# Projections and causal convolution of the next tile moved into the level steps of a gated delta layer

## The chip, the cores and the metric

The kernel runs on one core of one Trainium2 chip. The metric is the device time of one launch in microseconds. The unchanged kernel takes 6232.35 us, the median of 3 runs (6223.12 to 6238.5).

## The reference

Two residual blocks work on x of shape (4, 1024, 128) in fp32. The first is a gated delta attention with 6 heads, keys and queries of 128, values of 32. The second is a stack of 6 layers of local attention and a feed-forward part, which the change doesn't touch. The part that the change touches computes, for the normalised x:

```python
q = _causal_conv_silu(x @ Wq, conv_q)   # depthwise, 4 taps over time, then silu
k = _causal_conv_silu(x @ Wk, conv_k)
v = _causal_conv_silu(x @ Wv, conv_v)
beta = sigmoid(x @ Wb); g = -exp(A_log) * softplus(x @ Wa + dt_bias)
q = _l2norm(q) * DK ** (-0.5); k = _l2norm(k)
def step(S, inp):                        # over the 1024 positions
    q_t, k_t, v_t, g_t, b_t = inp
    S = S * exp(g_t)
    u = (v_t - einsum('bhk,bhkv->bhv', k_t, S)) * b_t
    S = S + k_t * u
    return S, einsum('bhk,bhkv->bhv', q_t, S)
o = o * rsqrt(mean(o * o) + EPS) * norm_w * silu(x @ Wg)
x = x + o @ Wo
```

The projections have 768 + 768 + 192 columns, which are 14 chunks of up to 128 channels.

## The kernel before, in words

`delta_layer` handles the 1024 positions in 8 tiles of 128 positions by 4 batches, so that most operands are 128 partitions by 512 columns. A loop over t from -1 to 8 builds one block of instructions for each engine, and a barrier of all engines (line 899) ends each block. The block t = -1 only normalises tile 0. The block t = 8 only finishes tile 7. The eight blocks between do one tile each. `behind` (t >= 1) means that the output of the tile before is still to be projected and added; `ahead` (t < 7) means that the next tile's x is to be loaded, turned and normalised.

The order within a block is written out by hand, and each engine works through its own list in order. Semaphores tie the lists together. In this account "head of a tile" is everything up to the first level step:

- PE projects the 14 chunks of the convolution (line 316) into four banks in turn. ACT copies each chunk into `pre` behind three columns kept from the tile before (line 523), and writes the last tap to `cv` (line 531). DVE adds the other three taps (line 735), two chunks interleaved. ACT applies silu (line 536). POOL's `tensor_copy` puts the kept columns in front of a chunk (line 639) and keeps the new ones (line 642). In between, the old tile's output is scaled (`squares_o`, `gated_o`, lines 686 to 695), turned and projected (`turn_o`, `output`), added (`residual`, line 699) and normalised (`mean_1`, `variance(LAST_LN)`).
- PE computes the gates (line 322), ACT applies silu to them (line 552) and changes its table to Ln and Exp (line 555). DVE then works off a chain of small dependent operations for the decay and beta (lines 750 to 776, called the gate chain here; line 761 is the first that needs ACT's exponentials, L561). Behind it stand the masked decays (line 781) and the 12 scalings of q and k (line 791).
- POOL squares q and k (line 649), PE sums them (line 342).

Then follow three pairs of heads. For a pair, the inverse of a 128 by 128 triangular matrix is built in six levels i = 1 to 6. At each level and for each of the two heads (x = 0, 1), PE forms one product (line 412, four matrices, each an fp32 product of two instructions), ACT copies it (`p1`, line 614), PE forms two further products (lines 433 and 436), and DVE subtracts them from `tr` and `tt` (lines 854 and 856). POOL prepares the masked blocks `ao` (line 660), up to two levels early. It waits for `at_ready` at level 1 of a pair and for an earlier product of line 412 at the others. In pairs 0 and 1, levels 1 and 3 also hold the decay products of the next heads (lines 352, 353), levels 2 and 4 their key products (lines 362, 363), and DVE `weigh`s them after levels 2 and 4 (lines 802 to 810). DVE's `first_t` (lines 817, 822) comes before level 6. In pair 2 the same slots hold `turn_x`, `mean_x` and `variance(NEXT_LN)`.

Between two pairs lies a passage: PE reads the states (lines 443, 445), turns A of the next heads (`turn_a`, line 370, taken to `at` by ACT, line 573), and waits for DVE's `r_ready` (lines 873 to 877) before the product of line 455. Then come the outputs and state updates (lines 463, 465), `turn_k` (line 376), and the next pair's first product of line 412.

## Time and profile before

The profiled execution took 6223.25 us, its span 6221.4 us. The delta layer occupies the span up to about 2280 us.

| what | value |
|---|---|
| PE busy | 5319.4 us, 86% of the span |
| DVE busy | 4155.1 us, 67% |
| ACT busy | 2763.5 us, 44% |
| POOL busy | 2394.6 us, 38% |
| mean granted TensorE clock | 0.924 of full speed |
| delta layer, tiles start (t = 0 to 8) | 27.9, 296.4, 578.6, 859.5, 1141.8, 1422.7, 1705.0, 1985.9, 2267.0 us |

Busy times are sums over the engine's instructions. The tile starts are the first table loads of line 501 after each barrier. The span in slices shows PE at five to eight tenths in the delta layer and at nine tenths behind it, with a granted clock of seven to nine tenths in the first part. PEclk is given in tenths or as a share; 1.00 is 2.4 GHz and 0.50 is 1.2 GHz.

### The profile page before, as it was taken

The page shows a single profiled execution, that of the slowest core. Times are in us where ns is not written, and L with a number is a line of the kernel's source. Part 1 is how long each engine was busy: PE and PEld are TensorE (multiplying, and loading weights), DVE is VectorE, ACT ScalarE, POOL GpSimd, SP SyncE. Part 2 cuts the span into 40 slices and gives each one's busy share as a digit, 9 for nine tenths or more (in the row PEclk, how much of TensorE's full clock was granted, in tenths as well). Part 3 has the DMA queues.
Part 4 walks back from the last instruction along what each step waited for, and adds up shares of the span by engine and source line. Part 5 has one row for each costly group of instructions (what it writes and reads, how often), then busy time and mean ns, then how long its engine had stood idle before and what let it go on. Part 6 is the DMA issues. An engine that isn't in the chain of part 4 may idle for free. (4 is left out here: it accounts for less than half of the span.)

```text
span 6221.4 us, 170219 instructions
## 1 busy us (share of the span) xinstructions
PE 5319.4 (86%) x71376; PEld 3399.9 (55%) x71376; DVE 4155.1 (67%) x6338; ACT 2763.5 (44%) x5037; POOL 2394.6 (38%) x2148
## 2 busy tenths in 40 slices
PE   5878778686968768999999999999999999999994
PEld 4856657584857654444444555545444445445552
DVE  6565665556565657777777777777777777777772
ACT  4232231413132315555555555555555555555552
POOL 2232222222222215444444444444444444444440
PEclk8888888797878879999999999999999999999997
DMA  0000000000000002222222222222222222222221
GB/s 20 3 2 4 1 4 1 4 1 4 3 2 3 1 32 67 60 60 68 63 60 60 70 68 60 60 70 67 58 53 70 64 56 60 65 72 58 58 58 34
DMA packets 255841, 252.14 MB, mean 41 GB/s; under 512 B 29680, under 2 KB 248688, under 8 KB 254704
## 3 DMA queue, kind: packets, MB, share of 16 engines
q1 hardware_dynamic: 255088, 241.29, 15.4%
q8 instruction: 571, 9.36, 0.6%
q14 instruction: 182, 1.49, 0.1%
HBM read 29.90 MB, written 4.19 MB: 5 GB/s over the span
## 5 line engine op out<-in xcount | busy, mean ns | idle before, releaser
L1360 POOL TENSOR_TENSOR turn<-prod 128x512 f32<-128x512 f32 x768 | 983.0, 1280 | 1944.4 <-DVE prod L1400 1002.2
L1103 PE MATMUL banks<-w2s,xs 128*128 128x512 f32 x2304 | 1242.0, 622 | 97.2 <-DVE xs L1432 89.7
L1400 DVE TENSOR_TENSOR prod<-banks,tabs 128x1024 f32<-128x1024 f32 x768 | 935.6, 1218 | 114.1 <-ACT sq L1247 113.9
L1247 ACT ACTIVATE sq<-banks 128x512 f32<-128x512 f32 x768 | 458.6, 597 | 963.0 <-PE banks L1103 959.2
L1369 POOL TENSOR_TENSOR turn<-turn,rs 128x512 f32<-128x512 f32 x768 | 832.7, 1105 | 88.2 <-ACT rs L1264 84.2
L660 POOL TENSOR_TENSOR ao<-at,msk 128x512 f32<-128x512 f32 x288 | 388.0, 1358 | 1045.7 <-PE banks L412 564.2
L1133 PEld LDWEIGHTS banks<-msk,turn 128*128 128x128 f32 x3072 | 324.3, 140 | 572.4 <-issue 566.2
L1436 DVE TENSOR_REDUCE mx<-banks 128x8 f32<-128x512 f32 x384 | 265.5, 691 | 385.5 <-PE banks L1119 383.0
L1411 DVE TENSOR_REDUCE ss<-sq 128x8 f32<-128x512 f32 x768 | 518.8, 676 | 1.5
L854 DVE TENSOR_TENSOR tr<-tr,banks 128x512 f32<-128x512 f32 x240 | 165.1, 688 | 510.4 <-PE banks L436 509.1
L614 ACT ACTIVATE p<-banks 128x512 f32<-128x512 f32 x288 | 172.0, 597 | 722.4 <-PE banks L412 722.4
L1133 PE MATMUL banks<-msk,turn 128*128 128x128 f32 x3072 | 482.6, 280 | 3.4 <-ACT ot L1292 1.6
L1103 PEld LDWEIGHTS banks<-w2s,xs 128*128 128x128 f32 x2304 | 352.7, 193 | 149.8 <-DVE xs L1432 98.5
L1119 PE MATMUL banks<-kx,qt 64*32 64x64 f32 x24576 | 352.3, 224 | 89.1 <-issue 88.9
L412 PE MATMUL banks<-tr,ao 128*128 128x128 f32 x2304 | 345.9, 299 | 93.0 <-DVE tt L856 58.1
L1181 PE MATMUL banks<-ot,w2s 128*128 128x512 f32 x768 | 394.3, 595 | 3.8 <-ACT ot L1292 3.8
L1119 PEld LDWEIGHTS banks<-kx,qt 64*32 64x32 f32 x24576 | 274.2, 105 | 183.7 <-issue 183.4
L412 PEld LDWEIGHTS banks<-tr,ao 128*128 128x128 f32 x2304 | 308.2, 209 | 120.9 <-DVE tt L856 80.9
L1208 PE MATMUL banks<-xf,w2s 128*128 128x512 f32 (+1 forms) x576 | 296.9, 626 | 89.6 <-ACT msk L1321 59.7
L1286 ACT ACTIVATE pt<-banks 128x512 f32<-128x512 f32 x384 | 229.2, 597 | 311.6 <-PE banks L1140 311.6
L1158 PE MATMUL banks<-v,pt 64*32 64x66 f32 x24576 | 332.9, 225 | 2.7 <-ACT pt L1286 2.7
L1446 DVE RECIPROCAL rc<-banks 128x8 f32<-128x8 f32 x384 | 78.4, 204 | 382.5 <-PE banks L1158 382.4
(202 smaller groups left out, 9828.7 us busy)
## 6 DMA issues: line engine op xcount, KB each, us to landing
v<-v_tok SPq DMA_DIRECT2D x1152, 132.0 KB
v<-v_tok SPq DMA_DIRECT2D x384, 66.0 KB
v<-v SPq DMA_DIRECT2D x188, 132.0 KB, 2.5
w2s<-in_weights SPq DMA_DIRECT2D x10, 768.0 KB, 4.7
tabs<-in_rot SPq DMA_DIRECT2D x40, 128.0 KB, 2.7
w2s<-in_weights SPq DMA_DIRECT2D x1, 2713.5 KB, 11.0
w2s<-in_weights SPq DMA_DIRECT2D x10, 256.0 KB, 3.0
xin<-in_x SPq DMA_DIRECT2D x8, 256.0 KB, 2.9
```

Of the source, the lines that this page charges most:

```text
L412: last = pe.matmul(p[3 * x][:, b * P:(b + 1) * P], ao[:, 2 * x + i % 2, b, :], tr[:, x, b, :], start=True, stop=True)
L660: g.tensor_tensor(ao[:, 2 * x + i % 2, :, :], at[:, x, :, :], over_batches(msk[:, M_OFF + LEVELS + i, :]), ALU.mult)\
L1103: pe.matmul(a_bank(use), xs[:, t % 2, b * P:(b + 1) * P], w[:, at:at + 512], start=True, stop=True).then_inc(a_done, 1)
L1119: last = pe.matmul(sc[n * WIN:(n + 1) * WIN, h, b * 2 * WIN:(b + 1) * 2 * WIN], qt[r, j, b * P + n * WIN:b * P + (n + 1) * WIN], kx[r, j, ...
L1133: last = pe.transpose(turn_bank[:, i * P:(i + 1) * P], src[:, i * P:(i + 1) * P], ident)
L1158: last = pe.matmul(pv[n * WIN:(n + 1) * WIN, h, b, :], pt[r, g % 2, b * P + n * WIN:b * P + (n + 1) * WIN], v2[r, h2, b, n, i * DV1:(i + 1 ...
L1181: pe.matmul(out_bank, w[:, W_O + j * P:W_O + (j + 1) * P], ot[:, g % 3, :], start=(j == 0), stop=(j == NP2 - 1)).then_inc(o_done, 1)
L1247: a.activation(sq[:, r % 2, :], a_bank(use), ACT.Square).then_inc(sq_done, 1)
L1360: gp.tensor_tensor(turn[:, r % ROTS, :, :].rearrange(halves, s=2), prod[:, r % 2, 0, :, :].rearrange(halves, s=2), prod[:, r % 2, 1, :, :] ...
L1369: gp.tensor_tensor(turn[:, r % ROTS, :, :], turn[:, r % ROTS, :, :], along(rs[:, q % 2, b, :], DH), ALU.mult).then_inc(rot_done, 1)
L1400: v.tensor_tensor(prod[:, r % 2, :, :, :], a_bank(use).rearrange("p (h d) -> p h d", h=HU).unsqueeze(1) .to_broadcast([P, 2, HU, DH]), tab ...
L1411: v.tensor_reduce(ss[:, q % 2, b, :], sq[:, r % 2, :].rearrange("p (h d) -> p h d", h=HU), AX.X, ALU.add).then_inc(red_done, 1)
```

## The change

The 14 chunks of tile t + 1 are projected, taken, convolved and their last columns kept inside the level steps of tile t: chunk number `pair * 6 + i - 1`, so one chunk at each level until 14 are done (pair 2 has chunks 12 and 13). POOL handles chunk `pair * 6 + i - 2`, after its `ao` products of level i. The unactivated results stay in a second half of `acts`, and ACT applies silu to all 14 at the head of the next tile. The x of the next tile is turned and normalised in the head rather than in pair 2, and the old tile's output is scaled in the head (`squares_o`) and pair 1 (`gated_o`) and projected, added and normalised in pair 2. The chunks' banks are p[1] and p[4], so the product of line 433 goes to p[0] and p[3]. `pre` has two buffers for four. Tile 0's chunks are done in the block t = -1. The memset of `acts` is twice as wide, and that of `cv` goes. Several scratch tiles become views of others.

The diff, cut to what matters for the order and the waits:

```diff
-PRE = 4
+PRE = 2
...
         state = sb("state", [P, H1, NB, DV])
         xin = sb("xin", [P, NB, P])
...
-                v.memset(cv[:], 0.0)
+                v.memset(acts[:], 0.0)
                 v.memset(state[:], 0.0).then_inc(init_done, 1)
...
             attend, behind, ahead = 0 <= t < NT, t >= 1, t + 1 < NT
-            LAST_LN, NEXT_LN = 1, 1 + behind
+            NEXT_LN, LAST_LN = 1, 1 + ahead
+            act_qkv, conv = acts[:, t % 2, :, :], acts[:, (t + 1) % 2, :, :]
+            o, o_old = os[:, t % 2, :, :], os[:, (t - 1) % 2, :, :]
...
+                    def project(n):
+                        m = P if n < NCH - 1 else VD - P
+                        if n == 0:
+                            pe.wait_ge(xn_ready, 1)
+                        if n >= 2:
+                            pe.wait_ge(tap_ready, n - 1)
+                        pe.matmul(p[CONV_BANKS[n % 2]][0:m, :], w[:, n * P:n * P + m], xn[:], start=True, stop=True)\
+                            .then_inc(proj_ready, 1)
 
...
+                            for n in range(NCH):
+                                project(n)
...
-                    for n in range(NCH):
-                        m = P if n < NCH - 1 else VD - P
-                        if behind and n == 4:
-                            turn_o()
-                        if behind and n == 6:
-                            output()
-                        if behind and n == 8:
-                            mean_1()
-                        if n >= 4:
-                            pe.wait_ge(tap_ready, n - 3)
-                        pe.matmul(p[n % 4][0:m, :], w[:, n * P:n * P + m], xn[:], start=True, stop=True)\
-                            .then_inc(proj_ready, 1)
...
+                    if ahead:
+                        turn_x()
+                        mean_x()
+                        variance(NEXT_LN, p[2])
 
                     pe.wait_ge(silu_ready, NCH)
-                    if behind:
-                        pe.wait_ge(rstd_ready, LAST_LN)
                     for b in range(NB):
...
+                    if ahead:
+                        pe.wait_ge(xn_ready, 1)
+                    pe.wait_ge(ln_done, NQK)
...
-                            elif ahead and pair + 1 == H1 // 2:
+                            chunk = pair * (LEVELS - 1) + i - 1
+                            if ahead and chunk < NCH:
+                                if i <= 2 and pair:
+                                    pe.wait_ge(u_taken, 2 * pair)
+                                project(chunk)
+                            if behind and pair + 1 == H1 // 2:
                                 if i == 1:
-                                    turn_x()
+                                    turn_o()
                                 elif i == 2:
-                                    mean_x()
-                                elif i == 4:
-                                    variance(NEXT_LN, p[6])
+                                    output()
+                                elif i == 3:
+                                    mean_1()
+                                elif i == 5:
+                                    variance(LAST_LN, p[7])
                             for x in range(2):
...
-                                        pe.matmul(p[3 * x + 1][:, b * P:(b + 1) * P], tt[:, x, b, :],
+                                        pe.matmul(p[3 * x][:, b * P:(b + 1) * P], tt[:, x, b, :],
...
+                            if ahead:
+                                pe.wait_ge(tap_ready, min(NCH, (pair + 1) * (LEVELS - 1)))
...
-                    for n in range(NCH + PRE):
-                        if behind and n == 4:
-                            take_o()
-                        if behind and n == 10:
-                            square(LAST_LN)
-                        if n < NCH:
-                            take(n)
-                        if n >= PRE:
-                            silu(n - PRE)
-                        if n < NCH:
-                            last_tap(n)
+
...
                     a.wait_ge(gates_ready, 1)
                     for i in range(2):
                         src = p[4 + i][:, 0:2 * GW].rearrange("p (b n) -> p b n", b=2)
                         a.activation(sg[:, t % 2, 2 * i:2 * i + 2, :], src[:, :, 0:VD], ACT.Silu)\
                             .then_inc(gates_taken, 1)
-                    a.wait_ge(silu_ready, NCH)
+                    for n in range(NCH):
+                        a.activation(act_qkv[:, n, :], act_qkv[:, n, :], ACT.Silu).then_inc(silu_ready, 1)
+                        if ahead and n == 3:
+                            take_x()
+                        if ahead and n == 9:
+                            square(NEXT_LN)
                     a.preload_act_table_set(LN_EXP)
-                    if behind:
-                        rstd(LAST_LN, p[7])
+                    if ahead:
+                        rstd(NEXT_LN, p[2])
 
...
+                    if ahead:
+                        a.wait_ge(xn_ready, 1)
...
-                            if ahead and not more:
+                            chunk = pair * (LEVELS - 1) + i - 1
+                            if ahead and chunk < NCH:
+                                take(chunk)
+                                last_tap(chunk)
+                            if behind and pair == 1 and i == 1:
+                                inverse_o()
+                            if behind and not more:
                                 if i == 1:
-                                    take_x()
-                                elif i == 3:
-                                    square(NEXT_LN)
-                                elif i == 5:
-                                    rstd(NEXT_LN, p[6])
+                                    take_o()
+                                elif i == 4:
+                                    square(LAST_LN)
+                                elif i == 6:
+                                    rstd(LAST_LN, p[7])
...
+                    if not attend:
+                        if ahead:
+                            for n in range(NCH):
+                                keep_tail(n)
+                        return
...
+                            chunk = pair * (LEVELS - 1) + i - 2
+                            if ahead and 0 <= chunk < NCH:
+                                keep_tail(chunk)
...
+                    def convolve(n):
+                        m = P if n < NCH - 1 else VD - P
+                        v.wait_ge(pre_ready, n + 1)
+                        v.wait_ge(front_ready, n + 1)
+                        v.wait_ge(tap_ready, n + 1)
+                        dst = blocks(conv[0:m, n, :])
+                        for tap in range(KS - 1):
+                            if tap:
+                                v.wait_ge(conv_step, n * (KS - 2) + tap)
+                            v.scalar_tensor_tensor(dst, pre[0:m, n % PRE, :, tap:tap + P], cw[0:m, n, tap:tap + 1],
+                                                   dst, ALU.mult, ALU.add)\
+                                .then_inc(conv_step if tap < KS - 2 else conv_ready, 1)
...
+                            for n in range(NCH):
+                                convolve(n)
+                            v.wait_ge(conv_ready, NCH)
...
-                    for pair in range(0, NCH, 2):
-                        v.wait_ge(pre_ready, pair + 2)
-                        v.wait_ge(front_ready, pair + 2)
-                        v.wait_ge(tap_ready, pair + 2)
-                        for tap in range(KS - 1):
-                            for n in (pair, pair + 1):
-                                m = P if n < NCH - 1 else VD - P
-                                if tap:
-                                    v.wait_ge(conv_step, tap_count(n, tap - 1))
-                                dst = blocks(cv[0:m, n % PRE, :])
-                                ins = v.scalar_tensor_tensor(dst, pre[0:m, n % PRE, :, tap:tap + P],
-                                                             cw[0:m, n, tap:tap + 1], dst, ALU.mult, ALU.add)
-                                ins.then_inc(conv_step if tap < KS - 2 else conv_ready, 1)
-                        if behind and pair == 0:
-                            gated_o()
-                        if behind and pair == 4:
-                            residual()
-                        if behind and pair == 6:
-                            centre(LAST_LN, x1[:])
-                    v.wait_ge(conv_ready, NCH)
...
+                    if ahead:
+                        v.wait_ge(xt_ready, 1)
+                        centre(NEXT_LN, xt_new, p[3])
+                        normed(NEXT_LN, blocks(xn[:]))
+                    if behind:
+                        squares_o()
...
-                    if behind:
-                        normed(LAST_LN, last_block())
...
-                                    v.tensor_tensor(tr[:, x, :, :], tr[:, x, :, :], blocks(p[3 * x + 1]),
+                                    v.tensor_tensor(tr[:, x, :, :], tr[:, x, :, :], blocks(p[3 * x]),
...
+                            chunk = pair * (LEVELS - 1) + i - 1
+                            if ahead and chunk < NCH:
+                                convolve(chunk)
+                            if behind and pair == 1 and i == 4:
+                                gated_o()
+                            if behind and not more:
                                 if i == 2:
-                                    v.wait_ge(xt_ready, 1)
-                                    centre(NEXT_LN, xt[:, (t + 1) % 2, :])
-                                elif i == LEVELS - 1:
-                                    normed(NEXT_LN, blocks(xn[:]))
+                                    residual()
+                                elif i == 3:
+                                    centre(LAST_LN, x1, p[7])
+                                elif i == 6:
+                                    normed(LAST_LN, last_block())
```

## Rows read from the trace of the kernel before

**Rows 1.** The table by stretches, tile 4; columns: stretch, length, busy times, PEclk.
```profile
1141.84:1191.80 49.96, 25.35 (x52) 11.27 (x53) 37.18 (x58) 32.41 (x57) 14.81 (x30) 0.70 0.04 11
1191.80:1243.74 51.94, 34.22 (x118) 20.85 (x118) 34.96 (x69) 20.99 (x37) 16.44 (x14) 0.73 0.00 0
1243.74:1306.08 62.34, 55.76 (x432) 54.32 (x433) 38.55 (x66) 11.02 (x19) 17.18 (x13) 0.88 0.00 1
```

**Rows 2.** Timeline, end of tile 4's head; columns: start, length, engine, line, operation.
```profile
1189.02 1.28 ACT L555 ACT_TABLE_LOAD   x1
...
1191.81 0.45 PE L332 MATMUL banks<-msk,act_qkv 128*128 128x128 f32 x1 [14.37 <-ACT lrs L483]
...
1192.11 0.18 DVE L761 TENSOR_SCALAR t<-t 128x24 f32<-128x24 f32 x1 [1.07 <-ACT t L561]
```

**Rows 3.** Timeline, start of the kernel, first block and first tile.
```profile
2.66 6.03 DVE L227 MEMSET act_qkv<- 128x7168 f32 x1 [1.44 <-issue]
...
18.75 2.08 PE L271 MATMUL banks<-xt,msk 128*128 128x512 f32 x2 [0.69 <-ACT xt L489]
...
24.45 0.69 ACT L482 ACTIVATE llg<-banks,cst 128x512 f32<-128x512 f32 x1 [2.17 <-PE banks L275]
...
67.21 0.18 DVE L761 TENSOR_SCALAR t<-t 128x24 f32<-128x24 f32 x1 [0.59 <-ACT t L561]
```

**Rows 4.** Groups by line in the delta layer; columns: shapes, count, busy, mean ns.
```profile
L536 ACT ACTIVATE act_qkv<-cv 128x512 f32<-128x512 f32 x112 | 70.3, 628 | 36.0 <-DVE cv L735 34.6
...
L322 PE MATMUL banks<-w1s,xn 128*128 128x204 f32 x64 | 12.5, 338 | 0.0
...
L688 DVE TENSOR_TENSOR sg<-sg,rows 128x768 f32<-128x768 f32 x8 | 7.6, 948 | 0.0
```

**Rows 5.** Line 735's instructions: duration in ns, minimum, median, maximum.
```profile
L735 DVE SCALAR_TENSOR_TENSOR cv<-pre,cw,cv x336: 733/745/1531, 33.0 to 2030.4; 128x512 f32<-128x512 f32 x168
```

**Rows 6.** Timeline of PE, a level without extras, then a 512-column product.
```profile
1283.79 1.06 PE L412 MATMUL banks<-tr,ao 128*128 128x128 f32 x8
1285.33 1.16 PE L412 MATMUL banks<-tr,ao 128*128 128x128 f32 x8 [0.48 <-DVE tt L856]
...
1289.90 1.06 PE L412 MATMUL banks<-tr,ao 128*128 128x128 f32 x8
...
1378.21 1.02 PE L271 MATMUL banks<-xt,msk 128*128 128x512 f32 x2
1379.07 1.05 PE L433 MATMUL banks<-p,tt 128*128 128x128 f32 x8
```

**Rows 7.** Timeline of PE, the wait in level 3 of pair 0.
```profile
1268.30 0.77 PE L352 MATMUL banks<-msk,gm 128*128 128x128 f32 x2 [3.83 <-DVE pm L810]
```

**Rows 8.** Timeline of DVE: weighing under POOL's product, weighing alone, next operation.
```profile
1263.17 1.55 DVE L802 TENSOR_TENSOR pm<-gat,msk 128x512 f32<-128x512 f32 x1
...
1285.19 0.69 DVE L802 TENSOR_TENSOR pm<-gat,msk 128x512 f32<-128x512 f32 x1
...
1288.31 0.69 DVE L854 TENSOR_TENSOR tr<-tr,banks 128x512 f32<-128x512 f32 x1
```

**Rows 9.** Timeline, passage from pair 0 to pair 1.
```profile
1294.20 1.28 DVE L859 TENSOR_TENSOR tt<-tt,banks 128x512 f32<-128x512 f32 x2
...
1298.44 1.08 ACT L573 ACTIVATE at<-banks 128x512 f32<-128x512 f32 x2 [5.21 <-PE banks L370]
...
1299.12 5.84 POOL L660 TENSOR_TENSOR ao<-at,msk 128x512 f32<-128x512 f32 x4 [19.17 <-ACT at L573]
...
1306.08 2.38 PE L412 MATMUL banks<-tr,ao 128*128 128x128 f32 x16
```

**Rows 10.** The table by stretches, 4 us each, narrow products at both clocks.
```profile
1298.00:1302.00 4.00, 4.00 (x39) 4.00 (x37) 2.95 (x9) 1.08 (x2) 2.88 (x3) 1.00 0.00 0
1410.00:1414.00 4.00, 4.00 (x20) 4.00 (x21) 1.92 (x8) 0.00 (x0) 0.00 (x0) 0.50 0.01 4
```

**Rows 11.** Timeline of PE, products of line 455 at the lower clock.
```profile
1410.01 3.60 PE L455 MATMUL banks<-r,tt 128*128 128x32 f32 x16
```

More of the change, by code:

```diff
@@ L265, in turn_x @@
                         for b in range(NB):
[L266 to L281 removed]
+                            pe.transpose(p[6][:, b * P:(b + 1) * P], o_old[:, b, 0:P], ident)
+                            last = pe.transpose(p[7][0:VD - P, b * P:(b + 1) * P], o_old[:, b, P:VD], ident)
                         last.then_inc(on_turned, 1)
@@ L631, in _, with keep_tail @@
                 def _(g):
-                    if not attend:
-                        return
-                    for n in range(NCH):
+                    def keep_tail(n):
                         m = P if n < NCH - 1 else VD - P
@@ L706, in _ @@
                             v.wait_ge(xt_ready, 1)
[L707 removed]
+                            centre(NEXT_LN, xt_new, p[3])
                             normed(NEXT_LN, blocks(xn[:]))
+                            for n in range(NCH):
+                                convolve(n)
+                            v.wait_ge(conv_ready, NCH)
                         if behind:
```

126 lines of the change are left out of this document (53 added, 73 removed).

## The prediction

> **What bounds the kernel now.** I read the table by stretches first. In tile 4 the head up to the first transpose of v takes 50.0 us, the rest of the head 51.9, the first of the three pairs 62.3 [rows 1]. PE is busy half the time in the first stretch, and 55.8 of 62.3 us in a pair. So the head is bound by chains over DVE and ACT, the pairs by PE. The timeline shows what ends the head's first part: PE's transposes of v wait 14.37 us for ACT, and DVE's gate chain passes its wait for the exponentials (line 761) at 1192.11, 50.3 us after the tile began [rows 2]. All behind it is ordered by that chain. In the pairs, a level without extras takes 1289.90 - 1283.79 = 6.11 us, of which PE waits 0.48 us for `tt` [rows 6]; level 3 of pairs 0 and 1 has a wait of 3.83 us for `pm` [rows 7].
>
> **The change, part by part.** S is a tile's start. Seven tiles (t = 0 to 6) have the next tile's chunks.
>
> *Head.* New order: gates at the cold clock, 8 x 0.338 = 2.7 us [rows 4]; table load 1.28 [rows 2]; two silus of the gate, 0.85; 14 silus, each 0.628 long and 0.52 apart as ACT operations overlap by about 0.1, 7.3 [rows 4]; `take_x` and `square` between them, 1.0. That is S + 13.4. The load back, 1.3, then Ln and Exp, 1.35 (0.69 for the first, [rows 3]): S + 16.1. The variance product, 2.08 us when cold [rows 3], is done beside the last silus. DVE then multiplies xn (0.7) and does `squares_o`, three operations of 0.95 [rows 4], which stood beside PE's start before and now stand ahead of line 761. I add 0.5 for collisions with POOL's squares. Line 761 comes at S + 20.2, not S + 50.3: 30.1 us gained, and 0.6 more as `normed(LAST_LN)` leaves DVE's list, less rounding, 30.5. DMAs: SP issues the x load at the same place, but its data are now needed behind the gates' 2.7 us on PE rather than in pair 2, about when they land; the store of x1 moves from the head into pair 2, and SP's list holds nothing else. In tile 0 line 761 stood at 67.21 - 27.89 = 39.3 [rows 3] and comes at S + 17: 22.3 gained. Tile 7 has no x to normalise: S + 14, 36.8 gained.
>
> *A chunk in a level.* PE: one 512-column product is 1379.07 - 1378.21 = 0.86 us, with its gap 0.9 [rows 6]. ACT: two copies, 1.1 us; it is idle most of a pair (11.0 busy of 62.3, [rows 1]). DVE: three dependent taps of 0.745 plus 0.02, 2.3 us [rows 5]. After `tt` DVE has about 4 us until the next deltas, so the taps are hidden in levels 1, 2 and 4, which pay PE's 0.9: 4.5 us a tile (levels 1, 2 and 4 of pair 0, 2 and 4 of pair 1).
> The trace has the same kind of operation with two operands in SBUF under POOL's products: 1.55 us where alone it is 0.69 [rows 8]. The bound for a chunk is thus 2.3 to 4.7 us. I take 2.3, since POOL now waits inside `keep_tail` for ACT's copy in the middle of the level, and its `ao` products move to where DVE reads PSUM. The rule of the Trainium skill ("SBUF — State Buffer", section on who interferes with whom) says that a DVE instruction with two SBUF inputs and a GpSimd instruction that reads SBUF block each other for the whole instruction; the trace agrees (1.55 against 0.69), and by it alone each chunk would be at the upper bound.
>
> *Level 3.* `weigh` took 1268.30 - 1263.17 = 5.1 us under POOL's products and 3.1 alone [rows 7, 8]. With POOL displaced it takes the short time, PE's wait falls from 3.83 to about 2, and the following products may stay at the high clock. With the chunk's 0.9 included I expect -2.6 (ends -3.3 and -1.0): -5.2 a tile.
>
> *The passages, the point that decides.* DVE's `convolve(5)` waits for `front_ready(6)`. POOL's `keep_tail(5)` stands behind the two `ao` products of level 1 of the **next** pair, and these wait for `at_ready`, that is for PE's state products, `turn_a` and ACT's copy. Queued behind the waiting `convolve(5)` on DVE are the r operations, and PE's line 455 waits for them. Before, the passage ran without a gap on PE: from the level-5 product at 1283.79 to the next pair's at 1306.08, 22.3 us [rows 6, 9], DVE's last `tt` at 1295.5, `at` taken at 1298.4 and POOL starting at 1299.1 [rows 9]. New, counted from T5, that level-5 product: `weigh` 1.3 to 4.4, `convolve(3)` to 6.6, `tt` of level 5 to 9.0, `convolve(4)` to 11.3, `first_t` to 14.2, `tt` of level 6 at 15.4 (before 11.7). PE ends the states at 16.2, `turn_a` 17.1; `at` 17.4; two `ao` of 1.27 to 20.0 [rows 9]; front copy 20.2. The taps now collide with the next two `ao` and end at 24.0; r is ready at 25.1 and 26.0, where it was at 15.3. PE stands for 8 us. The clock then decides: line 455's 16 instructions take 3.6 us at 0.50 [rows 11]. Warm, the next pair begins at T5 + 33.6; cold throughout, at 37.2. In level 1 the decay products no longer wait for DVE. Cold: T2 of pair 1 comes 15.0 later than before; warm: 10. The second passage carries `gated_o` too (1.9 us on the same DVE list, two of 0.95) and `turn_o`, and is 18.0 later cold, 13.3 warm. I take cold: in the tile's end the same narrow products run at 0.50 through 4 us in which PE was busy all the time [rows 10]; at 1298 they ran at 1.00, after levels that had run at 1.00 too.
> The Trainium skill ("TensorE: Matmul & The Clock Gate", "What's actually happening") says that the default state is throttled and activity releases it. By that rule the work after the stall would bring the clock back inside the passage, which is rival B below; the stretch at 0.50 speaks against it here.
>
> *Pair 2.* `output` for `mean_x` in level 2 with the last chunk, +1.8. In level 3 `mean_1` waits for the residual, which is queued behind `convolve(13)`: 2.3 + 0.9, +3.2. The variance only moves. Together +5.0.
>
> *Start.* The memset doubles, 12.1 for 6.03, and cv's 2048 columns (1.7 at the same rate) go: +4.3 [rows 3], and ACT waits for it. The 14 chunks in the block t = -1 have nothing beside them: lead-in 3.2, then 14 x 2.3 on DVE, 35.4. Together +39.7.
>
> *Sum.* Tiles 1 to 6: -30.5 + 4.5 - 5.2 + 15.0 + 18.0 + 5.0 = +6.8 each, +40.8. Tile 0: 28.6 in the pairs (33.0 without `gated_o`, `turn_o` and the variance, with the levels' -0.7) - 22.3 = +6.3. Tile 7: -36.8 + 5.8 for the old tile's work = -31.0. Start +39.7. Total +55.8 on the profiled 6223.25 us: 6279. That execution lies at the bottom of the three runs, whose median is 9 us higher; I put the forecast at 6283.
>
> **The rivals.** *A, the stall does not occur* (front copies early, or r not held up): each passage is then 11 us shorter (the 8 us of the stall and 3 of the cold products behind it), 14 times: -154, 6129. For it: POOL is idle 62% of the span. Against it: the written order, where the copy stands behind a wait that ended 19.17 us after POOL's last work [rows 9]. It decides on the side of faster. *B, the clock returns in the passage*: 5 us less, 14 times, 6213. For it: narrow products at 1.00 [rows 10]. Against it: the same rows at 0.50. *C, the taps collide with `ao` inside the levels*, as in the block above on its upper bound: 1.6 us more on the four chunks of a tile where DVE has no slack (3 and 4 of pair 0, 9 and 10), 7 tiles: +45, 6328. For it 1.55 against 0.69 [rows 8]. Against it POOL's displacement. *D, the head keeps most of its length* because the 14 silus and two layer-norm steps wait on each other: 5 us less gained in 8 tiles, 6323.
>
> **How the numbers follow.** The likeliest case has 0.50, A 0.10, B 0.17, C 0.13, D 0.10. A measurement tells about 0.3% from no change here, 6214 to 6251. A is faster; half of B is faster and half the same; of the main case 0.04 is faster and 0.10 the same, as the errors of its terms (about 4 us a tile) reach there. That gives faster 0.10 + 0.08 + 0.04 = 0.22, same 0.08 + 0.10 = 0.18, slower 0.60. The range 6190 to 6335 takes in B with level 3 at its better end, C and D, and leaves out A and little else.
>
> **What would show it.** A tile period near 288 us in tiles 1 to 6 (now 281). Line 761 about 20 us after a tile's start. Before the first tap of chunks 5 and 11 DVE waits some 5 us for POOL's copy, and PE's line 455 waits some 8 us for DVE's r; their clock is 0.50. The block t = -1 ends 35 us later. I am wrong if line 455 follows `turn_a` closely, if taps in the levels last over 1 us, or if the head's gain is not near 30 us.

## The result: 1% slower

The changed kernel took 6288.70 us (median of 4 runs, 6286.06 to 6295.83), the kernel before 6227.74 us (median of 4, 6217.35 to 6238.50) beside it. The ratio is 1.010, 95% interval 1.0083 to 1.0117. The forecast was 6283.

The second layer's code is the same in all kernels here and took 3951.6 to 3973.6 us in the profiled executions, whatever was changed in the first. So I compare profiles by the end of the delta layer, the first table load of the second layer: 2267.0 us before, 2331.2 after, 64.1 us later. The medians are 61.0 us apart. One run of e7 below took 9139.85 us at a granted clock of 0.864, where its others had 0.927 to 0.930, and is left out of that kernel's numbers.

Tile 4 by PE's timeline, in us; "states" is the first product of line 450 (443 before), "next pair" the first product of line 412:

| part of tile 4 | before | after | difference |
|---|---|---|---|
| tile start to first level of pair 0 | 101.90 | 68.55 | -33.35 |
| levels of pair 0, to its states | 50.54 | 53.25 | +2.71 |
| states to pair 1 | 11.80 | 24.76 | +12.96 |
| levels of pair 1 | 49.94 | 54.73 | +4.79 |
| states to pair 2 | 12.07 | 24.76 | +12.69 |
| levels of pair 2 | 38.12 | 48.04 | +9.92 |
| states to the next tile | 16.44 | 16.05 | -0.39 |
| tile | 280.81 | 290.14 | +9.33 |

The kernel before has two kinds of tile, and tile 4 is one of them. In its tiles 1, 3 and 5 the head takes 98.2 to 98.3 us and the second passage 17.47, in tiles 2, 4 and 6 they take 101.9 and 12.07; the tiles last 282.3 to 282.4 and 280.8 us. Against the mean of tiles 1 to 6 the change gains 31.9 us in the head, loses 13.0 and 10.0 in the two passages and 16.9 in the levels of the three pairs, and a tile is 8.4 us longer.

What the changed kernel waits for, first. The next lines are from its view of waits over the delta layer (us in total, times, longest); neither stood in a passage before.

```profile
PE banks L464 <- issue: 115.1, 14, 8.2
...
DVE acts L721 <- issue: 77.4, 14, 6.4
```

Fourteen times is twice a tile in the seven tiles with chunks of a next one. "issue" says only that no finished instruction explains the wait. The timeline of the passage from pair 0 to pair 1 names the cause (start, length, engine, line, operation; [rows 9] is the same place before):

```profile
1339.64 1.09 ACT L568 ACTIVATE at<-banks 128x512 f32<-128x512 f32 x2 [4.57 <-PE banks L368]
...
1340.32 2.48 POOL L665 TENSOR_TENSOR ao<-at,msk 128x512 f32<-128x512 f32 x2 [13.09 <-ACT at L568]
1342.74 0.20 POOL L640 COPY pre<-tail 128x12 f32<-128x12 f32 x1
...
1343.03 4.08 DVE L721 SCALAR_TENSOR_TENSOR acts<-pre,cw,acts 128x512 f32<-128x512 f32 x3 [4.90 <-issue]
...
1343.15 3.41 POOL L665 TENSOR_TENSOR ao<-at,msk 128x512 f32<-128x512 f32 x2
...
1348.26 3.59 PE L464 MATMUL banks<-r,tt 128*128 128x32 f32 x16 [8.22 <-issue]
1351.67 0.61 PE L472 MATMUL banks<-u,pm 128*128 128x32 f32 x2
...
1360.24 2.65 PE L412 MATMUL banks<-tr,ao 128*128 128x128 f32 x16
```

Read it downwards. POOL works on the next pair once `at` is there, and only then makes the 0.20 us front copy of chunk 5. DVE has stood 4.90 us for that copy, with the r operations behind it. PE stands 8.22 us for r, after which everything runs at the lower clock. The table by stretches gives that clock in the column behind the busy times (1.00 is 2.4 GHz, 0.50 is 1.2 GHz):

```profile
1335.40:1340.00 4.60, 4.60 (x43) 4.40 (x41) 2.65 (x4) 0.36 (x1) 0.00 (x0) 1.00 0.00 0
1340.00:1348.00 8.00, 0.04 (x1) 0.00 (x0) 4.83 (x7) 0.73 (x2) 6.79 (x7) 0.58 0.00 0
1348.00:1352.00 4.00, 3.74 (x18) 3.77 (x18) 1.74 (x8) 0.00 (x0) 0.00 (x0) 0.50 0.00 0
1352.00:1360.20 8.20, 8.20 (x40) 8.20 (x40) 5.08 (x15) 0.57 (x1) 0.00 (x0) 0.50 0.01 2
1360.20:1368.90 8.70, 8.70 (x68) 8.22 (x67) 2.38 (x8) 4.39 (x10) 2.49 (x3) 0.91 0.00 0
```

The head, in the timeline of tile 4 ([rows 2] before):

```profile
1213.68 1.28 ACT L542 ACT_TABLE_LOAD   x1 [15.85 <-PEq L905]
...
1228.71 0.69 DVE L688 TENSOR_TENSOR xn<-xc,rs 128x512 f32<-128x512 f32 x1 [6.46 <-ACT rs L492]
...
1232.93 0.90 DVE L763 TENSOR_SCALAR t<-t 128x24 f32<-128x24 f32 x1
```

The gate chain (line 763, was 761) begins 19.25 us into the tile and not 50.27 us: 31.0 us gained. The change's purpose is thus met in full. In tile 4 the passages take back 25.7 us of it and the levels of the pairs 17.4.

### The profile page after: what moved, and what is told of

Its sections match the earlier page's. It is cut to its first block and busy times, and to the rows that moved or that the text cites. A ratio compares the mean times of both kernels' runs of the same rounds, so it can differ in the third digit from the quotient of the medians.

```text
span 6294.0 us, 170281 instructions
## 1 busy us (share of the span) xinstructions
PE 5385.5 (86%) x71376; PEld 3462.0 (55%) x71376; DVE 4125.3 (66%) x6337; ACT 2746.3 (44%) x5029; POOL 2349.0 (37%) x2148
## 5 line engine op out<-in xcount | busy, mean ns | idle before, releaser
L721 DVE SCALAR_TENSOR_TENSOR acts<-pre,cw,acts 128x512 f32<-128x512 f32 x336 | 287.3, 858 | 88.8 <-issue 77.4
```

## The experiments

Each kernel was run against the kernel before on the same chip. Not all rows are from one chip. "Layer end" is the first table load of the second layer in the profile; lines shift by up to 7 in the variants.

| kernel | median us (range, runs) | ratio to before, 95% | layer end us |
|---|---|---|---|
| changed kernel | 6288.70 (6286.06 to 6295.83, 4) | 1.010, 1.0083 to 1.0117 | 2331.2 |
| e1, early copy | 6195.54 (6195.05 to 6203.10, 4) | 0.9952, 0.9935 to 0.9968 | 2238.3 |
| e2, late taps | 6124.87 (6120.81 to 6126.80, 4) | 0.9832, 0.9816 to 0.9849 | 2168.3 |
| e3, busy wait | 6253.07 (6245.80 to 6263.08, 5) | 1.0042, 1.0027 to 1.0056 | 2289.2 |
| e4, no chunks | 6041.99 (6034.78 to 6049.19, 2) | 0.9701, 0.9679 to 0.9724 | 2073.7 |
| e5, head | 6268.75 (6262.65 to 6280.98, 6) | 1.007, 1.0056 to 1.0083 | 2309.2 |
| e8, residual first | 6094.42 (6089.28 to 6100.31, 5) | 0.9784, 0.9771 to 0.9797 | 2122.3 |
| e6, schedule | 6094.08 (6085.11 to 6100.96, 5) | 0.978, 0.9766 to 0.9795 | 2131.0 |
| e7, e6 and e5 | 6074.76 (6059.06 to 6081.21, 5) | 0.9744, 0.973 to 0.9759 | 2114.2 |
| e9, wide between | 6059.56 (6054.32 to 6068.81, 4) | 0.9729, 0.9706 to 0.9751 | 2097.9 |
| e10, narrow between | 6129.50 (6124.85 to 6129.93, 4) | 0.9834, 0.9812 to 0.9855 | 2164.4 |
| e11, e7 and wide, two places | 6050.76 (6046.97 to 6053.07, 5) | 0.9707, 0.9694 to 0.972 | 2080.8 |
| e12, wide in three places | 6049.07 (6044.46 to 6053.68, 5) | 0.9708, 0.9695 to 0.9721 | 2090.0 |

### e1: POOL makes the copy of chunks 5 and 11 at the end of their own pair

```diff
-                            if ahead and 0 <= chunk < NCH:
+                            if ahead and i > 1 and chunk < NCH:
                                 keep_tail(chunk)
+                            if ahead and i == LEVELS - 1 and chunk + 1 < NCH:
+                                keep_tail(chunk + 1)
```

> The changed kernel, but POOL handles chunks 5 and 11 at the end of level 6 of their own pair, before its products for the next pair, instead of behind them. The order theory (DVE's taps of chunks 5 and 11 wait for POOL's front copy, which is queued behind products that wait for the next pair's A, and the r operations wait behind the taps): the 8.2 us stall of PE shrinks to about 2 us, the products behind it run at the high clock, each passage is some 11 us shorter, 14 passages, so about 6135 us (6115 to 6165). The rival, that the passages are long because DVE has 4.6 us more taps in levels 4 and 5 and the copy is beside the point: at most 3 us a passage, 6245 us or more.

93 us below the changed kernel, 6.6 us a passage: the written order of the copy costs that much. It is not the 11 us that the theory had: the time lies between the theory's range and the rival's, so the copy's place is a part of the cause and not the whole. In tile 4 states to next pair took 20.44 us in the first passage and 14.83 in the second (24.76 both in the changed kernel). The timeline of the first shows what replaced the wait:

```profile
1288.45 5.07 POOL L665 TENSOR_TENSOR ao<-at,msk 128x512 f32<-128x512 f32 x4 [5.50 <-ACT at L568]
...
1289.90 1.23 DVE L885 TENSOR_TENSOR r<-r,t 128x128 f32<-128x128 f32 x1
...
1291.23 1.89 PE L464 MATMUL banks<-r,tt 128*128 128x32 f32 x8 [3.06 <-issue]
...
1295.48 0.61 PE L472 MATMUL banks<-u,pm 128*128 128x32 f32 x2
```

The taps still stand ahead of r, which now meets POOL's `ao` (1.23 us for an operation that takes 0.29 alone), PE waits 3.06 us and its narrow products run at 0.50 again.

### e2: the taps of chunks 5 and 11 behind r, u and the copy of t on DVE

```diff
-                            if ahead and chunk < NCH:
+                            if ahead and chunk < NCH and i < LEVELS - 1:
                                 convolve(chunk)
...
                             for x in range(2):
                                 first_tt(2 * pair + 2 + x)
+                            if ahead:
+                                convolve(pair * (LEVELS - 1) + LEVELS - 2)
```

> The changed kernel, but DVE works off the taps of chunks 5 and 11 behind the u and first_tt operations of the passage instead of ahead of the r operations; POOL's order stays as it is. Order theory: r no longer waits, the passage is about 12 us shorter, 14 times, 6120 us (6095 to 6160), somewhat under the early copy, since these taps leave the path too. The rival (it is the amount of DVE work that counts): the taps are merely done later, at most 3 us a passage, 6245 us or more. If only POOL's products of the next pair were late, this would change nothing, 6289 us.

Measured 6124.87, 164 us less than the changed kernel or 11.7 us a passage, and 1.7% less than before. POOL's order is untouched here; what is gone is that r was queued behind the waiting instruction. States to next pair took 11.62 and 12.38 us in tile 4, as in the same tile before the change (11.80, 12.07). Over tiles 1 to 6 the passages gave 25.1 us a tile and the levels of pair 1 took 2.5 of them back: without the stall PE waits in level 1 again (2.54 us in tile 4). PE's products of line 464 follow at the high clock and without a wait:

```profile
1246.69 1.87 PE L464 MATMUL banks<-r,tt 128*128 128x32 f32 x16
...
1253.91 2.33 PE L412 MATMUL banks<-tr,ao 128*128 128x128 f32 x14
```

### e3: PE keeps busy with 32 unused products while it waits

```diff
                                 turn_a(2 * pair + 2 + x)
+                            if ahead:
+                                pe.wait_ge(tri_ready, 2 * pair + 1)
+                                for _ in range(32):
+                                    pe.matmul(p[2][:, 0:P], le, le, start=True, stop=True)
```

> The changed kernel with 32 further 128x128 products on PE in each passage (tiles 0 to 6), into a bank that is free there, placed in the stall before line 464; they leave the result as it is. They take 7.1 us at the high clock, within the 8.2 us stall. If the low clock behind the stall comes from PE standing still, it stays at 1.00 through the products of lines 464 to 474, 3.6 us less a passage, 14 times: about 6238 us (6225 to 6255). If the narrow products themselves bring the clock down whatever stood before them: within 15 us of the changed kernel, 6275 to 6295 us.

36 us less (2.5 a passage), at the upper end of the first range. The stretches of the first passage: state products, the 32 wide products, line 468 to the first narrow ones, the rest of the narrow ones.

```profile
1307.00:1311.20 4.20, 4.20 (x41) 4.20 (x40) 2.42 (x4) 0.19 (x1) 0.00 (x0) 1.00 0.00 0
1311.20:1318.60 7.40, 7.36 (x66) 7.17 (x64) 4.11 (x4) 0.90 (x2) 6.83 (x7) 1.00 0.01 2
1319.60:1322.90 3.30, 3.23 (x28) 3.18 (x28) 2.52 (x9) 0.00 (x0) 0.00 (x0) 1.00 0.00 0
1323.30:1328.80 5.50, 5.50 (x27) 5.50 (x28) 3.60 (x12) 0.53 (x1) 0.00 (x0) 0.50 0.00 0
```

The standing does cost the clock: without it line 468's products (464 in the changed kernel) ran at 1.00, 2.10 us for the sixteen against 3.59. But the clock then fell amid 128x32 products, after 3.3 us in which PE had been idle for 0.07. So the low clock has a second cause.

### e4: no chunk in any level

```diff
-                            if ahead and chunk < NCH:
-                                if i <= 2 and pair:
-                                    pe.wait_ge(u_taken, 2 * pair)
-                                project(chunk)
...
-                            if ahead and chunk < NCH:
-                                take(chunk)
-                                last_tap(chunk)
...
-                            if ahead and 0 <= chunk < NCH:
-                                keep_tail(chunk)
...
-                            if ahead and chunk < NCH:
-                                convolve(chunk)
```

> The changed kernel with the 14 chunks of the levels left out (projection, copies, taps, kept columns) in tiles 0 to 6: the next tile's q, k and v are not computed. What is left is the new head and the old tile's output in pairs 1 and 2. If the head's gain of 33 us and the levels' loss are separate sums, a tile takes about 252 us (281 - 33 + 4), 7 tiles, so about 6025 us (6000 to 6060). If the head's gain depends on work that is only shifted, the tile stays above 260 us, 6080 us or more.

This kernel leaves out the next tile's q, k and v. Measured 6041.99. Its tiles 1 to 6 have a period of 251.0 us against 281.6 before and 290.0 in the changed kernel. So the change without its chunks (the new head, with the old tile's output moved into pairs 1 and 2) is worth 30.6 us a tile, and the chunks in the levels cost 39.0 us a tile, of which e2 gets back 22.9 by one place in DVE's list.

### e5: another order in the head

```diff
-                    if ahead:
-                        rstd(NEXT_LN, p[2])
-
                     a.wait_ge(e1_asked, 1)
                     for i in (3, 4, 5):
                         a.activation(t24[:, i + 3, :, :], t24[:, i, :, :], ACT.Exp).then_inc(e1_ready, 1)
+                    if ahead:
+                        rstd(NEXT_LN, p[2])
...
-                        normed(NEXT_LN, blocks(xn[:]))
...
                     link(v.tensor_tensor(BETA, S1, E_BM, ALU.mult))
+                    if ahead:
+                        normed(NEXT_LN, blocks(xn[:]))
```

> The changed kernel with another order in the head of a tile alone: ScalarE takes the three exponentials ahead of rstd of the next tile's norm, and VectorE puts squares_o ahead of normed and normed behind the product BETA. What it tests: that the first product of the gate chain (line 763 of the changed kernel, 19.25 us into the tile) stands behind VectorE's 6.46 us wait for rstd, and that the whole tile follows that chain. Theory: line 763 comes some 4 us earlier in each of the seven tiles with a next one and nothing gives it back, 6288.7 - 28 = about 6261 us (6250 to 6272). Rival: the norm, now behind BETA, is late for the rest of the head (its 8 products and the scalings take the place it left), and the time is 6280 to 6295.

20 us less, 2.9 in each of seven tiles of the 4 expected. The chain does begin 5.1 us earlier in tile 4 (at 14.12 us), but the first scaling of q and k (line 792) stands at 27.55 us and not 30.15: half is lost between them.

```profile
1216.00 0.18 DVE L762 TENSOR_SCALAR t<-t 128x24 f32<-128x24 f32 x1 [2.84 <-ACT t L553]
...
1217.26 0.69 DVE L688 TENSOR_TENSOR xn<-xc,rs 128x512 f32<-128x512 f32 x1 [0.53 <-ACT rs L492]
...
1219.28 1.02 DVE L776 TENSOR_SCALAR t<-t 128x24 f32<-128x24 f32 x1
1220.33 0.18 DVE L775 TENSOR_TENSOR t<-t 128x24 f32<-128x24 f32 x1
...
1219.23 1.04 POOL L654 TENSOR_TENSOR sq<-acts 128x512 f32<-128x512 f32 x1 [10.72 <-PE banks L340]
```

Six of the chain's steps, 0.18 us each alone, take 0.91 to 1.02 beside POOL's squares, which last 1.04: 4.7 us in excess. In the changed kernel it was five, at 0.64 to 0.96, 3.3 us in excess. With normed's 0.6, which is now inside the chain, that is 2.0 of the 2.5 us lost.

### e8: e2, and the residual ahead of the chunk's taps in the last pair

```diff
+                            if behind and not more and i == 2:
+                                residual()
                             if ahead and chunk < NCH and i < LEVELS - 1:
                                 convolve(chunk)
```

> The kernel with the last chunk's taps behind the copy of t (e2_late_taps, 6124.9 us) and one thing more: in level 2 of the last pair VectorE adds the residual ahead of a chunk's taps and not behind them. What it tests: level 3 of the last pair took 12.2 us in the changed kernel and 6.11 before, 3 us more than the term of the prediction; in its trace the taps of the last chunk (4.00 us for three) stand ahead of the residual, which the centring products on TensorE wait for. Theory: the order of the two costs 3 to 5 us in each of six tiles, so 6125 - 24 = about 6101 us (6092 to 6110). Rival: the taps run slowly because GpSimd's copies run beside them, whatever the order, and the residual then collides in their place: 6118 to 6130 us.

30 us less than e2 (46 us by the layer's end). In the changed kernel (first fence) PE waits for the residual behind three slow taps; in e8 (second fence) it does not, though the taps are still slow:

```profile
1459.51 4.00 DVE L721 SCALAR_TENSOR_TENSOR acts<-pre,cw,acts 64x512 f32<-64x512 f32 x3
1463.43 0.68 DVE L707 TENSOR_TENSOR xin<-banks,xt 128x512 f32<-128x512 f32 x1
...
1464.16 2.08 PE L292 MATMUL banks<-xin,msk 128*128 128x512 f32 x2 [3.36 <-DVE xin L707]
```

```profile
1321.28 0.68 DVE L707 TENSOR_TENSOR xin<-banks,xt 128x512 f32<-128x512 f32 x1
1322.00 3.29 DVE L721 SCALAR_TENSOR_TENSOR acts<-pre,cw,acts 64x512 f32<-64x512 f32 x3
...
1322.42 1.02 PE L292 MATMUL banks<-xin,msk 128*128 128x512 f32 x2
```

That level took 12.02 us in e2 and 6.97 here. Over tiles 1 to 6 it accounts for 36 of the 46 us. Part of the rest is clock: in tiles 4 and 5 level 3 of pair 0 took 12.55 us in e2 and 10.89 here with the same wait of 1.9 us in it; in tile 4 the clock behind that wait read 0.77 and 1.00. In the other four tiles it took 12.5 us in both.

### e6 and e7: the chunks dealt 4, 4, 6; and with e5's head

```diff
+            CHUNKS = (range(0, 4), range(4, 8), range(8, NCH))
...
-                            chunk = pair * (LEVELS - 1) + i - 1
-                            if ahead and chunk < NCH:
+                            chunk = CHUNKS[pair].start + i - 1
+                            if ahead and chunk in CHUNKS[pair]:
...
+                        if ahead:
+                            convolve(CHUNKS[pair][-1])
```

e6 has e8's edits too. POOL's copies of a pair's chunks now all stand inside that pair, so the fault of the changed kernel is gone from its list as well.

> Like the kernel before it in this list (last taps of a pair behind the copy of t, residual ahead of the taps), and the 14 chunks dealt 4, 4 and 6 over the three pairs, where the change deals 6, 6 and 2: levels 5 and 6 of the first two pairs, at whose end VectorE and GpSimd are late, hold no chunk, and the last pair has six levels with one. Theory: what is left of the passages goes (the levels 4 to 6 of these pairs run as before the change, some 2 to 4 us a pair) and the last pair, whose levels are held by TensorE, takes 0.9 us for each of four more chunks, which leaves 2 to 4 us a tile: 6101 - 21 = about 6080 us (6060 to 6098). Rival: the last pair also carries the residual, the centring and the norm of the output, and four more chunks of taps make VectorE late there: 6105 to 6135 us.

> e6_schedule and e5_head together. Theory: the head and the levels are in series and their gains add: e6's time less 28 us, about 6052 us (6035 to 6070), which is 2.8% under the kernel before and 3.8% under the changed one. Rival: the head's order shifts GpSimd's squares into the passages or levels and part of it is lost: under 10 us between e6 and this one.

e6 gained nothing over e8. It missed its theory by 14 us, within the range stated. Its level parts did what was expected: level 5 to the states takes 10.5 and 11.6 us in pairs 0 and 1 of tile 4 (12.8 and 16.3 in e8). Four more chunks made the levels of pair 2 3.3 us longer, as expected. But the second passage, in which PE's list is unchanged, took 17.6 us for 12.6. PE was busy for all of it:

```profile
1285.00:1290.00 5.00, 5.00 (x37) 5.00 (x37) 2.97 (x10) 0.19 (x1) 0.00 (x0) 0.76 0.00 0
1290.00:1302.20 12.20, 12.20 (x59) 12.20 (x59) 8.21 (x18) 1.56 (x3) 5.54 (x5) 0.50 0.01 2
```

A low clock in this passage is not new with the edits. The kernel before has it there in tiles 1, 3, 5 and 7, where the passage takes 17.47 us, and not in tiles 2, 4 and 6, where it takes 12.07. Its tile 3 (first row) and tile 4 (second row):

```profile
1077.00:1089.20 12.20, 12.20 (x59) 12.20 (x59) 6.04 (x15) 1.55 (x3) 4.94 (x4) 0.50 0.01 2
1360.00:1364.00 4.00, 4.00 (x39) 4.00 (x38) 2.91 (x10) 1.09 (x2) 3.15 (x3) 1.00 0.01 4
```

e7 is 19 us under e6, as e5 was 20 under the changed kernel, and lies between its theory (28) and its rival (under 10). By tiles the two gains differ. e5's head is 3.1 to 3.6 us shorter in each of tiles 1 to 6. Between e6 and e7 the head gives 0.2 us in tiles 3 and 4 and 2.9 to 3.7 in the other four, and in tile 2 the first passage gives 4.4 more, since it ran at the low clock in e6 (17.28 us) and takes 12.86 in e7. So the sum came out at about e5's size, but not by adding in each tile.

### e9 and e10: wide products between the narrow ones, and a control

```diff
+                                if ahead and pair == 1 and b % 2 == 0:
+                                    pe.matmul(p[3 * x][:, 2 * P:3 * P], le, le, start=True, stop=True)
                                 pe.matmul(p[3 * x][:, b * DV:(b + 1) * DV], act_qkv[:, H1 + h, s],
                                           state[:, h, b, :], start=True, stop=True)
```

Two lines of the same kind stand ahead of the u products and the output products; e10 has `le[:, 0:DV]` as the second operand.

> e6_schedule (6094 us) with 12 products of 128x128 more in the second passage of each of seven tiles, one ahead of every second step of the state, the u and the output products, results unused. What it tests: in e6_schedule PE had no idle time from 1285 to 1302.2 in that passage, and yet its clock was 0.76 and then 0.50, and the passage took 17.6 us where before the change it took 12.1. Theory: 128x32 products do not hold the high clock even back to back, wide ones between them do. Then the clock in the passage reads 1.00, some 5 us of slow products go, the 12 cost 12 x 0.23 = 2.7 us (32 of them took 7.31 us in e3_busy_wait), and the time is 6094 - 7 x 2.3 = about 6078 us (6065 to 6092). Rival: the clock falls after a stretch of full use whatever the shape. Then it reads 0.50 again, the 12 cost up to 5 us, and the time is 6110 to 6135.

> The control for e9_wide_between: the same 12 places, products of 128x32 instead of 128x128. Theory (the shape decides): the clock in the passage stays at 0.50 and the 12 cost about 12 x 0.21 = 2.6 us, 6094 + 18 = 6112 us (6100 to 6125). If extra products of any shape bring the clock back, the time is under 6090 us, as in the wide one.

Twelve unused products of 128x128 in the passage made the kernel 34.5 us faster than e6, the same number of 128x32 made it 35.4 us slower, twice the 18 of its theory. The passage took 13.27 us in e9 and 22.69 us in e10. Their stretches, e9 first:

```profile
1265.40:1270.00 4.60, 4.60 (x44) 4.60 (x43) 2.29 (x7) 0.00 (x0) 0.00 (x0) 1.00 0.00 0
1270.00:1278.60 8.60, 8.60 (x80) 8.60 (x79) 6.59 (x13) 1.25 (x3) 6.00 (x5) 1.00 0.02 3
```

```profile
1302.80:1309.00 6.20, 6.20 (x45) 6.20 (x45) 2.56 (x7) 0.00 (x0) 0.00 (x0) 0.74 0.00 0
1309.00:1325.40 16.40, 16.40 (x79) 16.40 (x79) 8.01 (x21) 1.69 (x3) 5.08 (x5) 0.50 0.01 1
```

PE is busy throughout in both. What it did before the clock fell is the difference: 128x32 products in the extra places, or 128x128 ones. That settles that the kind of product decides here whether the clock falls. e9's gain was twice its theory's (34.5 for 16): the mean of tiles 1 to 6 fell by 5.4 us against 2.3 expected. The passage gave 4.2 of it, net of the twelve products, and level 1 of pair 2 behind it another 1.3 (7.09 us for 8.25 in tile 4).

### e11 and e12: the repairs together

e11 is e7 with `pair >= 1` in the condition above, e12 with no condition on the pair.

> e7_both (6075 us) with the 12 products of 128x128 of e9_wide_between in the second passage and also behind the last pair of each tile, which runs its narrow products at 0.50 as well. What it tests: whether the three repairs (late taps and dealt chunks, the head's order, wide products between narrow ones) add up, and whether the end of a tile gains like the passage. Theory: the passage gives back 34 us as it did in e9_wide_between, the tile's end 2 us in seven tiles, 6075 - 34 - 14 = about 6027 us (6010 to 6042). Rival: the tile's end is held by VectorE's steps of the state there and the 12 products cost 2.7 us in each tile: 6050 to 6065.

> e11_all (6050.8 us) with the 12 wide products in the first passage of each tile too. What it tests: e11_all came out 24 us above its theory, and its trace has the second passage at 13.27 us with the clock at 1.00 but the first, which has no wide products, at 17.28 us and 0.50, where e7_both had 12.91. Theory: the low clock had only moved to the passage without wide products; with them the first passage also takes 13.3 us, and the time is 6050.8 - 7 x 4.0 = about 6023 us (6012 to 6035). Rival: it moves on to the levels (their waits for VectorE in level 3), which then take 1.7 us more each: 6040 to 6056.

Both times lie in the rival's range. e11's rival was still wrong in its mechanism: the second passage took 13.27 us and the tile's end 14.03 (15.89 in e7), as the theory had it. But in tiles 3, 4 and 6 the first passage, without wide products, ran at the low clock and took 17.28 us, where e7 had 12.91; in tiles 1, 2 and 5 it took 12.7 to 12.8. Tile 4:

```profile
1188.40:1193.00 4.60, 4.60 (x39) 4.60 (x38) 2.92 (x9) 0.00 (x0) 0.00 (x0) 0.85 0.00 0
1193.00:1205.60 12.60, 12.60 (x61) 12.60 (x60) 8.91 (x21) 1.77 (x3) 5.54 (x5) 0.50 0.00 1
```

e12 mended that (13.27 us) and lost it next door: in tile 4 level 1 of pair 1 took 12.50 us for 9.47, and level 3 of pair 0 12.55 for 10.88. The two places trade. In all of tiles 1 to 6 of e6, e7 and e11, a level 3 of pair 0 of 10.88 us is followed by a first passage of 17.3, and one of 12.5 by a first passage of 12.6 to 13.1. Where the low clock falls moves with the edits, and in e6 and e11 from tile to tile; what a repair of one place gives can't be read from that place alone. Both are 2.9% under the kernel before (6050.76 and 6049.07).

## Why the prediction was right

The step on which it rested, the passages, held in mechanism and size. The stated range, 6190 to 6335, also takes in rivals B, C and D, so the time alone does not tell them from the likeliest case; the rows of the passages and e2 do. By its own cuts (tile 4; a passage runs here from the level-5 product to the second level of the next pair):

| term, us a tile | predicted | measured |
|---|---|---|
| head | -30.5 | -33.35 |
| chunks in levels held by PE | +4.5 | +3.7 |
| level 3, pairs 0 and 1 | -5.2 | -2.7 |
| first passage | +15.0 | +13.9 |
| second passage | +18.0 | +19.6 |
| pair 2 | +5.0 | +8.5 |
| end of the tile | 0 | -0.4 |
| sum | +6.8 | +9.3 |

I took every "before" from tile 4. Over tiles 1 to 6 the measured means are -31.9, +4.0, -3.0, +13.1, +17.2, +8.6 and +0.4, together +8.4. The second passage is the term for which tile 4 is least typical: in tile 3 it is +14.7, because that tile already had the low clock there.

- *Head.* Line 763 came at 19.25 us for 20.2; my terms up to the load back add up to 13.1 and not the 13.4 that I wrote, and that load came at 12.28. The scaling gained 2.2 us more than the chain, mainly since line 783's eight operations took 1.66 us there for 4.12: they no longer meet POOL's squares. I had not followed that collision of the old kernel. e4, which has everything of the change but the chunks, is 30.6 us a tile under the kernel before over tiles 1 to 6, with its head 31.9 shorter.
- *Chunks.* The taps took 2.32 us for three in levels 1, 2 and 4, so they hid, and rival C (collisions inside the levels) did not come about, save for one chunk of the last pair. There I had not asked where POOL stands (see *Pair 2*).
- *Level 3.* The wait fell from 3.83 [rows 7] to 1.89 us as forecast, and the first operation of the weighing from 1.55 to 0.69 [rows 8], but the products behind it stayed at the low clock (0.79 over that stretch). This is the term that I mis-sized: I took -2.6 each and got -1.6 and -1.1. e8 shows the good end, 10.89 for the 14.12 before, which is -3.2, when the clock is 1.00.
- *Passages.* DVE's wait of 4.90 (about 5), PE's of 8.22 (about 8), line 464 at 0.50, and 37.5 us from the level-5 product to the next pair (37.2) are all there. The stall needs both the copy's place in POOL's list and the taps' place in DVE's: moving the first took 6.6 us off a passage (e1), moving the second 11.7 (e2). In the second passage `gated_o` cost what I gave it: PE's wait ahead of level 6 is 2.67 us in pair 1 and 0.80 in pair 0, and the 1.87 between them are its two operations of 0.95, which stand on DVE from 1405.51 to 1407.45 with no idle time around them. Rival A (no stall) was the right price: 6129 forecast, 6124.87 in e2. Rival B (the clock comes back in the passage) fell: PE was busy for all of the 8.2 us in 1352.00:1360.20 at 0.50, and the clock came back only in the stretch of the next level, which reads 0.91. e9 against e10 shows that the kind of product matters. The Trainium skill says in "TensorE: Matmul & The Clock Gate", "What's actually happening", that the throttled state is the default and activity releases it. The trace does not agree that being busy is enough for that.
- *Pair 2.* The term was 3.5 us too small. I had the residual behind three taps at 2.3 us, but they took 4.00 beside POOL's `ao`, and PE's products behind the wait ran cold (2.08 for 1.02). With e8's order that level is 5.05 us shorter than in e2. The Trainium skill has in "SBUF — State Buffer", section on who interferes with whom, the rule that I weighed and set aside for the levels. Here the trace agrees with it (4.00 us for 2.32), as it does at the taps in the passage (4.08).
- *Outside the steady tiles.* Start +40.2 (39.7), tile 0 +7.6 (6.3), tile 7 -34.4 (-31.0). The six tiles between gave +50.6 (40.8), which is +8.4 a tile.

The sum for the layer was +55.8, measured 64.1 in the profile and 61.0 by the medians. In tile 4 the head came 2.9 us better than forecast, level 3 came 2.5 and pair 2 3.5 us worse, so one miss took back half of the two others. That the total is as close as this is partly luck.

Not settled: which stretches at the low clock a given edit moves, why the kernel before has them in the second passage of every other tile, and why in e1 the second passage (14.83 us) gained more than the first (20.43).

## What to carry to other kernels

When work is moved into a loop, look at the last piece of each round: if what releases it stands in the **next** round of another engine's list, everything queued behind it stands too. Put that piece behind the instructions for which the bound engine waits, here that one move leads from 1% slower to 1.7% faster. Then compare the clock of the stretches and not only their waits, since a PE that is busy with narrow products can run at half speed.

## What was not expected of the hardware

- PE's clock fell to 0.50 (1.2 GHz) in stretches in which PE had no idle time, amid 128x32 products (e6, and the kernel before in every other tile). The 128x128 turns of the same passage then ran at 0.50 too. With one 128x128 product ahead of every second step the clock stayed at 1.00 over 13.2 us; with 128x32 ones in the same places it read 0.74 and 0.50. Unused work made the kernel 34.5 us faster. The narrow products don't always bring the clock down: in e2 they ran at 1.00 from 1242.30 to 1250.00.
- The stretch at the low clock moves when it is mended in one place: in tile 4, e6 gave back 5.0 us in the second passage, e11 4.4 in the first, and e12 4.7 in two levels.
- An operation on 128x24 elements, 0.18 us long, takes up to 1.02 us when it starts beside one of POOL's 1.04 us products; so a chain of tiny operations can pay at many of its steps (six in e5, 4.7 us).
